# Graph attention and mixer network: six more units per layer turned in blocks by VectorE, and four reorderings in the first half

## The reference, cut to what matters

```
adj = zeros((N, N)).at[edge_index[0], edge_index[1]].set(1.0)       # first block, from edge counts
v   = x @ Wv + bv
...
q, k, v = split(x @ Wqkv, 3);  q, k = elu(q) + 1, elu(k) + 1         # mixer of the second block
kv  = einsum('bhnd,bhne->bhde', k, v)
...
for l in range(2):                                                   # second block, 8 heads of 64
    scores = einsum('ehd,ehd->eh', q[tgt], k[srcidx])
    p = exp(scores - segment_max(scores, tgt)[tgt])
    agg = segment_sum(p / s[tgt] * v[srcidx], tgt)
    x = batchnorm(x + agg @ Wo.T + bo);  x = batchnorm(x + ffn(x))
```

## Time and profile before

| | |
|---|---|
| executions | 1003.69 us median, 1000.15 and 1004.23 us the other two |
| profiled execution | 1001.43 us, its span 999.5 us |
| TensorE clock granted | 0.984 of full speed over the span |
| busy | PE 940.0 us (94%), VectorE (DVE) 632.2 (63%), ScalarE (ACT) 518.9 (52%), POOL 263.6 (26%) |
| layer 0 of the attention, 440 to 630 us | PE 187.28 us of 190 busy, DVE 129.92, ACT 123.36, DMA share 0.57 |
| layer 1, 706 to 896 us | PE 187.15 us of 190 busy, DVE 129.98, ACT 124.76, DMA share 0.54 |

### The profile page before, as it was taken

How to read it: one execution, slowest core, us unless ns; L and a number is a source line. 1 busy time by engine, 2 the same in 40 slices (tenths; PEclk the granted TensorE clock), 3 DMA queues, 4 the chain that set the end, 5 groups by cost and what they waited for, 6 DMA issues and landing times.

```text
span 999.5 us, 15408 instructions
## 1 busy us (share of the span) xinstructions
PE 940.0 (94%) x5418; PEld 688.5 (69%) x5426; DVE 632.2 (63%) x1096; ACT 518.9 (52%) x799; POOL 263.6 (26%) x140
## 2 busy tenths in 40 slices
PE   6999999999999999999999999999999999999825
PEld 2745545788887886887777767777777777777613
DVE  4776566567867424428676776466486676746795
ACT  1655353655735213408666676345476666653454
POOL 2000000399953051310000029313100000572700
PEclk9999999999999999999999999999999999999967
DMA  9201100000200121145655575111065555631102
GB/s 325 87 0 43 42 1 22 1 1 1 85 1 1 35 92 43 64 148 168 190 167 172 170 237 164 43 43 43 15 211 183 183 183 176 216 101 36 73 0 84
DMA packets 58849, 96.15 MB, mean 96 GB/s; under 512 B 8284, under 2 KB 38172, under 8 KB 58270
## 3 DMA queue, kind: packets, MB, share of 16 engines
q1 hardware_dynamic: 55454, 93.11, 28.8%
q10 hardware_dynamic: 3328, 2.15, 0.7%
HBM read 59.58 MB, written 33.55 MB: 93 GB/s over the span
## 4 chain that ended last, share of the span: by engine, by line
PE 85%; DVE 6%; issue 3%; ACT 2%; POOL 1%; DMA 1%; DVEq 0%; ACTq 0%; SPq 0%
PE slots L1905 75%; PE slots L1989 10%; DMA W<-in_wkT 1%; POOL X L749 1%; DVE XT L1601 1%; ACT X L1175 1%; DVE X L1790 0%; DVE XT L1638 0%; POOL WL L729 0%; DVE SM L1767 0%; ACT KRR L1107 0%; DVE KRL L1737 0%; DVE st L1753 0%; DVE PT L1856 0%; DVE st L1606 0%
## 5 line engine op out<-in xcount | busy, mean ns | idle before, releaser
L1905 PE MATMUL slots<-PT,XN 128*64 128x256 f32 x1024 | 117.6, 382 | 0.1
L1905 PE MATMUL slots<-KS,QS 64*128 64x512 f32 x768 | 107.4, 406 | 5.4 <-DVE nm L1688 5.1
L1688 DVE CUSTOM_DVE_ANT_0 SM<-slots,MASK 128x1024 f32<-128x1024 f32 x64 | 75.7, 1220 | 49.9 <-PE slots L1905 49.7
L774 POOL TENSOR_TENSOR QS<-QF,QS 128x512 fp32r<-128x512 f32 x16 | 20.7, 1294 | 314.5 <-ACT QS L1057 314.5
L1905 PEld LDWEIGHTS slots<-PT,XN 128*64 128x64 f32 x1024 | 71.5, 137 | 42.8 <-issue 11.3
L1905 PEld LDWEIGHTS slots<-KS,QS 64*128 64x128 f32 x768 | 72.8, 184 | 24.2 <-issue 11.3
L1041 ACT ACTIVATE SM<-SM,nm 128x1024 f32<-128x1024 f32 x64 | 73.3, 1146 | 26.8 <-DVE nm L1688 26.7
L823 ACT ACTIVATE PT<-slots 128x1024 f32<-128x1024 f32 x68 | 69.4, 1020 | 32.8 <-PE slots L1989 26.5
L1041 ACT ACTIVATE PT<-PT,nm 128x1024 f32<-128x1024 f32 x64 | 73.3, 1145 | 12.5 <-DVE nm L1688 11.2
L1905 PE MATMUL slots<-PT 128*128 128x512 bf16 (+3 forms) x384 | 76.6, 368 | 3.0 <-ACT PT L823 1.2
L1688 DVE CUSTOM_DVE_ANT_0 PT<-slots,MASK 128x1024 f32<-128x1024 f32 x64 | 75.2, 1211 | 4.1 <-PE slots L1905 3.9
(11 more groups left out here) (427 smaller groups left out, 2207.1 us busy)
## 6 DMA issues: line engine op xcount, KB each, us to landing
blocks<-FL SPq DMA_DIRECT2D x56, 512.0 KB, 3.3
PT<-blocks SPq DMA_DIRECT2D x224, 128.0 KB, 3.4
X<-in_x SPq DMA_DIRECT2D x4, 512.0 KB, 11.3
W<-in_wout SPq DMA_DIRECT2D x2, 1024.0 KB, 6.2
W<-in_gq SPq DMA_DIRECT2D x2, 1024.0 KB, 5.2
W<-in_gk SPq DMA_DIRECT2D x2, 1024.0 KB, 5.7
spill<-X SPq DMA_DIRECT2D x4, 512.0 KB, 2.6
SXR<-XTR SPq DMA_DIRECT2D x1, 2048.0 KB, 8.7
```

The lines of the kernel that those rows point to most:

```text
L774: nc.gpsimd.tensor_tensor(QS[:, j % 2, 1, :], QF[:], QS[:, j % 2, 0, :].bitcast(fp32), ALU.subtract).then_inc(q_split, 1)
L1688: nc.vector.tensor_tensor_reduce(out=SMs[n % SMB], in0=src, in1=MASK[:, unit(n)[2], :], scale=-1.0, scalar=-0.1 * NO_EDGE, op0=ALU.add, op ...
L1905: return nc.tensor.matmul(o_, lhsT, rhs, start=start, stop=stop)
```

## The change

`FLIPS` gains the even units 8, 16, 24, 32, 40 and 48 in both layers: they are flipped where they were turned. 28 flips a layer become 34; 12 turns and their 12 copies go, 12 VectorE transposes, 12 writes and 48 reads come. Besides: v0 1 is put ahead of kvT; the last tile of counts comes last in the first two adjT jobs; the first XTR rounding of the second mixer is cut in two halves, and v1 0 begins on the first; kv1 is ordered so that six tiles of two of its four column blocks come ahead of the last keys and values.

```diff
-FLIPS = [n for n in range(UNITS - 8) if n % 2 == 1]
+FLIPS = [n for n in range(UNITS - 8) if n % 2 == 1 or n % 8 == 0 and n > 0]
...
-    [("kvT", 0), ("v0", 1)],
+    [("v0", 1), ("kvT", 0)],
...
+                if n == 2 and j == 0:
+                    nc.scalar.activation(XTR[:, :, 0:P], src[:, :, 0:P], ACT.Copy).then_inc(first_tile_rounded, 1)
+                    nc.scalar.activation(XTR[:, :, P:2 * P], src[:, :, P:2 * P], ACT.Copy).then_inc(xT_rounded, 1)
+                    return
                 nc.scalar.activation(XTR[:, :, 2 * j * P:2 * (j + 1) * P], src, ACT.Copy).then_inc(xT_rounded, 1)
...
-                for dst, ts in tiles:
+                for hf, (dst, ts) in enumerate(tiles):
+                    if hf == 0:
+                        wait(first_tile_rounded, 1)
+                    else:
+                        wait(xT_rounded, 4 + j + 1)
...
-            need("counts", *range(TT))
-            for i in range(TT):
-                slot = begin("adjT", i)
-                for s in range(TT):
-                    last = turn(slot[:, s * P:(s + 1) * P], MASK[:, s, i * P:(i + 1) * P])
-                end(last)
+            def turn_counts(i, tiles):
+                for s in tiles:
+                    last = turn(slot_of("adjT", i)[:, s * P:(s + 1) * P], MASK[:, s, i * P:(i + 1) * P])
+                return last
+
+            need("counts", *range(TT - 1))
+            for i in range(2):
+                begin("adjT", i)
+                turn_counts(i, range(TT - 1))
+            need("counts", TT - 1)
+            for i in range(2):
+                end(turn_counts(i, [TT - 1]))
+            for i in range(2, TT):
+                begin("adjT", i)
+                end(turn_counts(i, range(TT)))
...
-            need("k1", 3)
-            need("v1", 3)
+            need("k1", 2)
+            need("v1", 2)
...
-                    for c in range(FC):
-                        for t in range(TT):
-                            last = mm(slot[:, 256 * c:256 * c + P + 2], K1[:, t, c * P:(c + 1) * P], V1[:, t, c, :], t == 0, t == TT - 1)
+                    for t, c in [(t, c) for pair in ((0, 2), (1, 3)) for t in range(TT) for c in pair]:
+                        if t == 6 and c == 0:
+                            need("k1", 3)
+                            need("v1", 3)
+                        last = mm(slot[:, 256 * c:256 * c + P + 2], K1[:, t, c * P:(c + 1) * P], V1[:, t, c, :], t == 0, t == TT - 1)
```

More of the change, by code:

```diff
@@ L462, in build @@
         v0_rounded, q0_rounded, p0_rounded = (sem(n) for n in ("v0_rounded", "q0_rounded", "p0_rounded"))
+        first_tile_rounded = sem("first_tile_rounded")
         xT_rounded, w_rounded, w_split, x_spilled, ffn_made, ffn_added, z_inverted, z_spread_act, z_spread_dve = (
@@ L1967, in split_token_major @@
                     if name == "v1" and j == 0:
-                        wait(xT_rounded, 4 + j + 1)
                         end(rests_last(slot, wr, wl, j))
```

## The result

| | median us | range, runs | ratio to before, 95% interval |
|---|---|---|---|
| before | 1003.38 | 1000.15 to 1004.61, 15 | |
| after | 995.84 | 992.32 to 1000.5, 15 | 0.9936 [0.9922, 0.9949] |

The change gains 7.5 us where the sum of the prediction had 14, and the time lies just outside the range (984.5 to 995.0). The runs of the kernel after spread over 8 us, those before over 4.5. The profiled execution is the slowest of the 15, 1000.5 us (span 998.8). Its granted clock, 0.979, is the lowest of the 15, against 0.985 in the median run, so the waits that it shows are probably longer than those of the median run, which was not profiled.

What follows compares the result with a forecast made beforehand. TensorE, busy 94% of the span, was taken as the bound. Terms of -11.4 - 0.8 - 1.1 + 0.1 - 0.8 = -14.0 us took 1001.43 to 987.4; adding 1.0 gave 988.4 us, range 984.5 to 995.

Steps and rivals of the forecast that it cites:

- The flips' gain: Attention: twelve turns leave TensorE's queue at 1.02 us each, 12.2 us; 11.4 after 0.8 for read-back waits.
- 16% more flips: Attention, VectorE: these extra flips cost nothing while their lateness is below 1.3 us.
- VectorE: Attention: its idle time covers the added flips, ready 0.2 us ahead of the scores, with 1.3 us of slot reserve.
- the wait for the FL buffer: Attention: the second flip of a pair waits 0 to 1.7 us for a write; costed at nothing, worst 2.4 in all.
- The read-backs: Attention aggregations: about 0.4 us of wait at one tightest place in each layer, 0.8 us in all.
- first half: The edits besides the flips (v0 1, adjT, XTR halves, kv1): a gain of 2.6 us together.
- The first rival: Attention: landings grow with load, twelve aggregations wait 0.8 us each, 9.6 us lost, time 996; chance 0.12.
- The slower rival: Attention: landings grow so much that the kernel is slower, 1008 us at a landing of 6.0; chance 0.04.
- VectorE as the pace: Attention: turns taken off TensorE come back as waits for VectorE; flips give nothing, time 999; chance 0.06.
- v0 and kvT: v0 1 ahead of kvT fills TensorE's 0.77 us idle for xmT: gain 0.8 us, bounds 0 and 0.8.
- adjT: Fourteen transposes put first cover TensorE's 1.17 us wait for the last counts copy: gain 1.1 us.
- kv1 and the halves: Second mixer: reordered kv1 starts q1 0 earlier, gain 0.8 us; XTR rounding in halves loses 0.1.

Runs made afterwards that it cites:

- e12: Kernel before plus only the six added flips a layer, load of go behind the reads of block 51, rounded behind exponential 60: 990.81 us, 0.9880.
- e6: Changed kernel with the 1 MB load of go issued two blocks later, behind the reads of block 51: 988.05 us, 0.9854.
- e9: Changed kernel with the load of go behind the reads of block 51 and ScalarE rounding it behind exponential 60 instead of 58: 986.33 us, 0.9836.
- e7: Changed kernel with the load of go in two 512 KB parts, behind the reads of 48 and of 51: 988.53 us, 0.9863.
- e2: Changed kernel with unit 48 of each layer turned by TensorE again: 989.73 us, 0.9878.
- e1: Changed kernel with the load of go three blocks later, behind the reads of block 53: 1006.34 us, 1.0052.
- e3: Kernel before with only the six added flips a layer: 1001.23 us, 0.9979.
- e5: Changed kernel with the load of go one block later, behind the reads of block 49: 1001.1 us, 0.9980.
- e8: Changed kernel with the load of go behind the reads of 53 and its rounding behind exponential 62 instead of 58: 996.92 us, 0.9953.
- e11: Kernel before with only its load of go moved between the write of 53 and the reads of 51: 1016.21 us, 1.0132.

## Why the prediction was wrong

**The flips' gain** was right: 1.02 us at a place in the rows; 11.1 us in the trace of e12 and 12.0 [10.1, 13.8] in its time, against 11.4. The "16% more flips" of the prediction is a slip, 34 against 28 are 21% more; no term hangs on it.

**VectorE** was right where it counts: the wait for the FL buffer came (0.76 us at 469.95) and made one masking about 0.4 us late, but TensorE's waits for VectorE's masking stayed at 5.1 us in all.

**The read-backs are the step that failed.** The sum had "For one such place in each layer I take off 0.8 us". I took the tightest of the aggregations right behind an added flip (1, 3, 5, 7, 9 and 11 of a layer), by distances in the kernel before, for flips and reads alone. Not one of these waited in the profile after. All five waits are at aggregations 0, 10 and 12, which the sum put at nothing; for the ones that take the added blocks the only reason was "The extra read-backs of unit 8 itself are in the queue two steps before they are wanted". SyncE's loop holds one more transfer, the load of go behind block 49, and I never asked what the added flip 48 does to the queue around it. It costs 9.2 us of waiting and 4.3 of clock in the profiled execution: 987.4 + 13.5 = 1000.9, and it took 1000.5. The stretch from the first aggregation to the last closes the same way: 437.0 us in the change (465.4 to 902.4), 423.5 in e12, 13.5 apart. In the median it costs 8 to 10 us (ratio 0.9936 against 0.9854 of e6 and 0.9836 of e9). That e6, the change with just the load moved, lands on the forecast of 988.4 is in part luck: it gains more in the first half than forecast and loses 2.8 us to waits for ScalarE (1.83 and 0.94) that the sum didn't have. The small waits were under-sized as well: 1.2 us here, 1.7 in e6, 2.2 in e9, against 0.8; that the 0.8 was near is luck too, as they fell at other places.

**The first rival** had the time (996) and the releaser, but another mechanism: landings longer everywhere, twelve waits of 0.8 us. The median write did grow (3.3 to 4.1 us, the page's list of DMA issues), the median read only from 3.4 to 3.6. Apart from the two long waits none is over 0.7 us. That its time came out is luck. The argument against it, by the order of the flips' own transfers ("these reads are queued ahead of the extra write"), left out the foreign one, the load. The slower rival and VectorE as the pace did not come. The write of 51 took 7 us more than usual, and e7 shows that this goes with the bytes ahead of it. The access time under high load that DMA: Bandwidth & Descriptors of the Trainium skill gives (section Latency and other measured facts) would, as an estimate (2 us less 0.2), have added 1.8 us. So it alone does not account for the 7 us paid here.

**The first half** gave 4.5 us (twice 0.9955), not 2.6. By the traces of e12 and e9: v0 and kvT 1.3 (forecast 0.8), adjT 1.3 (1.1), and kv1 and the halves 0.8 (0.7 together). In the kernel after, k1 0 waits for VectorE and q1 0 for POOL, as forecast, though k1 0 only 0.2 us longer than before (0.63 against 0.41) where 0.5 was said:

```profile
308.86 0.47 PE L1910 MATMUL slots<-WKR,XTR 128*128 128x512 f32 x1 [0.63 <-DVE SM L1511]
356.59 0.50 PE L1910 MATMUL slots<-XTR,WKR 128*128 128x512 f32 x1 [0.42 <-POOL WL L730]
```

The rest, 1.7 us between those two traces, is clock at one counts tile, in e12 and in e9:

```profile
149.42 7.07 PE L1906 MATMUL slots<-PT 128*128 128x512 bf16 x26
```

```profile
148.12 5.38 PE L1910 MATMUL slots<-PT 128*128 128x512 bf16 x26
```

TensorE did not wait ahead of it in either: it ran eight products of 34 rows for 3.7 us, and in e12 the granted clock then stood at 0.50 from 150 to 153 us. That tile is slow in three of four traces without the first half's edits and in one of ten with them; the tile at 93 us is slow (10.52 instead of 8.83) in none of four and in two of ten. In the mean that is 1.0 us in favour of the edits. Whether they cause it stays open with so few traces.

## What to carry to other kernels

When a change adds transfers to a queue, list everything that the queue issues near them, the odd weight load above all, and ask for each chained pair (a write, and the reads that wait for it) what now stands ahead of either. Here a large load that nobody waited for yet did best behind both, yet early enough for the engine that first touches it; where the two don't meet, splitting it (e7) and moving its user (e9) both worked. Price a wait of several microseconds on TensorE above its length, by the rows of the group behind it.

## What the runs showed of the hardware

- A write of 512 KB that usually lands in 3 to 4 us took 10.4 us when issued 0.5 us behind a 1 MB load, and 8.7 us at 1.4 us (layer 1). The load itself took 9.7 and 9.2 us instead of 5.0 before, with read-backs just ahead of it. Issued 2.7 us behind the load, in before and e2, the write took 3.8 and 4.2 us. Behind half the load (e7) it took 6.0 and 5.7.
- TensorE's waits of 1.43 and 1.83 us left the granted clock at 1.00 (2.4 GHz). Each wait of 2.99 to 7.19 us in these traces was followed by groups at 0.50 (1.2 GHz). Behind waits of 2.99 to 5.46 us this cost 1.5 to 2.9 us on the next aggregation, behind e1's two longer ones 1.3 us on the next scores and more on the turns. The clock can fall without a wait too: at the counts tile above the engine had been busy.
- The kernels with long waits spread more, but not all: after, e3, e5 and e8 over 7 to 13 us in 12 to 15 runs each; e6, e7 and e9, which have no long wait, over 2 to 5 in 5 runs each, and before over 4.5 in 15. e11 has long waits and a spread of 4 us in 5. Whether the waits themselves differ from execution to execution isn't shown, as each kernel has one trace.
